# Indirect DMA transfers of a seven-layer kernel, issued one by one behind other engines' steps instead of 32 in a row

## The reference

```python
x = L0_attn_x
x = x + _L0_attn_ref(_layernorm(x, axis=-1), ...)   # linear ("cosformer") attention and an MLP
x = x + _L0_ffn_ref(_layernorm(x, axis=-1), ...)    # channel mix
x = x + _L1_attn_ref(_layernorm(x, axis=-1), ...)   # latent attention, causal softmax
x = x + _L1_ffn_ref(_layernorm(x, axis=-1), ...)    # two groups of 32 experts, the top 2 of each
x = x + _L2_attn_ref(_layernorm(x, axis=-1), ...)   # attention with rotary factors
x = x + _L2_ffn_ref(_layernorm(x, axis=-1), ...)    # 8 experts, top 2
x = x + _L3_attn_ref(_layernorm(x, axis=-1), ...)   # state-space layer
x = x + _L3_ffn_ref(_layernorm(x, axis=-1), ...)    # attention over heads, 8 gated experts
```

```python
order = jnp.argsort(flat_e)
tok = flat_t[order]
xs = x2[tok]
...
return jnp.zeros_like(x2).at[tok].add(ys)
```

## Time and profile before

| | |
|---|---|
| median of 3 runs | 6739.3 us (6714.13 to 6750.03) |
| the profiled execution: its time, its span | 6708.75 us, 6707.2 us |
| granted TensorE clock, mean | 0.802 |
| busy: PE, DVE, ACT, POOL | 4840.0, 3601.1, 1805.1, 2175.1 us |
| one pair of the first loop | 327.5 us (scatters start at 408.97 and 736.42) |
| one pair of the second loop | 443.8 us (fetches start at 3294.80 and 3738.62) |

### The profile page before, as it was taken

One profiled execution on the slowest core, in us unless ns is written; L12 is line 12 of the kernel. 1 busy time (PEld: TensorE's weight loads), 2 busy tenths in 40 slices (PEclk: granted clock), 3 DMA queues, 4 the chain that ended last, 5 costly groups with the idle time before them and its releaser, 6 DMA issues. The chain is left out here.

```text
span 6707.2 us, 94963 instructions
## 1 busy us (share of the span) xinstructions
PE 4840.0 (72%) x36264; PEld 2885.3 (43%) x36264; DVE 3601.1 (54%) x10874; ACT 1805.1 (27%) x2589; POOL 2175.1 (32%) x2704
## 2 busy tenths in 40 slices
PE   4969696969696868667768677686686676876763
PEld 2444444444444444443544435334444353443442
DVE  2645454545454545447456475374664754746644
ACT  1324242423232323233113132131231322312310
POOL 2222222222222222546225243262242531623424
PEclk9979797979797979887778867777787777876885
DMA  4000000000000000650000000000000000000000
GB/s 144 1 20 1 21 1 20 1 20 3 19 4 17 4 17 4 201 163 7 16 10 2 15 10 7 14 7 16 10 4 13 10 9 12 7 16 10 4 13 3
DMA packets 142050, 147.57 MB, mean 22 GB/s; under 512 B 31150, under 2 KB 126065, under 8 KB 141065
## 3 DMA queue, kind: packets, MB, share of 16 engines
q1 hardware_dynamic: 114424, 94.58, 4.8%
q0 software_dynamic: 18432, 37.79, 1.9%
q10 hardware_dynamic: 8736, 8.91, 0.4%
HBM read 70.75 MB, written 62.59 MB: 20 GB/s over the span
## 5 line engine op out<-in xcount | busy, mean ns | idle before, releaser
L772 DVE CUSTOM_DVE_ANT_0 twin<-twin,w_mask_row 128x512 f32<-128x512 f32 (+3 forms) x2048 | 953.8, 521 | 387.1 <-PE twin L1696 384.4
L1696 PE MATMUL twin<-arena 32*128 32x128 f32 (+3 forms) x4096 | 843.9, 536 | 57.1 <-DVE arena L772 30.5
L1714 PE MATMUL twin<-arena 32*128 32x128 f32 (+3 forms) x4096 | 800.6, 512 | 36.5 <-DVE arena L772 35.3
L1393 ACT ACTIVATE arena<-twin 128x768 f32<-128x768 f32 (+1 forms) x544 | 477.9, 882 | 724.4 <-PE twin L1725 387.4
L1714 PEld LDWEIGHTS twin<-arena 32*128 32x128 f32 x4096 | 367.5, 208 | 488.6 <-issue 289.9
L684 POOL TENSOR_SCALAR ve<-mv 128x4 f32<-128x4 f32 x128 | 27.7, 217 | 1566.9 <-DVE mv L732 1566.3
L1696 PEld LDWEIGHTS twin<-arena 32*128 32x128 f32 x4096 | 373.2, 213 | 233.4 <-issue 115.2
L687 POOL TENSOR_SCALAR ve<-ssq 128x4 f32<-128x4 f32 x80 | 24.9, 311 | 1147.3 <-DVE ssq L1238 604.5
L1649 PE MATMUL twin<-w_ident,b 128*128 128x128 f32 x328 | 91.3, 434 | 377.1 <-DVE b L753 326.8
L308 POOL DMA_INDIRECT sorted_x<-got,w_mo_first_slots x288 | 291.1, 1011 | 112.6 <-issue 86.5
L1737 PE MATMUL twin<-arena 128*32 128x128 f32 (+3 forms) x2944 | 309.3, 463 | 3.2 <-POOL arena L592 3.2
(11 more groups left out here) (440 smaller groups left out, 10823.2 us busy)
## 6 DMA issues: line engine op xcount, KB each, us to landing
sorted_y<-arena SPq DMA_DIRECT2D x96, 256.0 KB, 2.7
sorted_x<-zeros ACTq DMA_DIRECT2D x2, 4096.0 KB, 20.0
a<-sorted_x SPq DMA_DIRECT2D x64, 128.0 KB
b<-sorted_x SPq DMA_DIRECT2D x64, 128.0 KB, 2.3
hres<-sorted_x SPq DMA_DIRECT2D x64, 128.0 KB
sorted_x<-got,w_mo_first_slots POOLq DMA_INDIRECT x288
got<-sorted_y,back POOLq DMA_INDIRECT x288
x_out<-w_l_w SPq DMA_DIRECT2D x18, 256.0 KB, 2.3
```

The costliest lines, as they stand in the source:

```text
L772: last = dve.tensor_tensor_reduce(s[:, e, at:at + w], s[:, e, at:at + w], W["mask_row"][:, T - w:T], -1.0, 3e38, ALU.add, ALU.min, into)
L1393: act.activation(at_pt[tag][n % len(at_pt[tag])][:, :, 0:w], twin[SLOT["scores_t", c, u] % 3][:, :, 0:w], ACT.Exp, scale=1.0 if tag == "l1 ...
L1696: last = pe.matmul(s[:, e, at:at + w], queries[r, P * i:P * (i + 1)], keys[r, 0:w], start=(at == 0), stop=True, skip_group_check=True)
L1714: last = pe.matmul(s[:, e, at:at + w], keys[r, P * m:P * (m + 1)], queries[r, P * m:T], start=(at == 0), stop=(tag == "l2"), skip_group_ch ...
```

## The change

The functions keep what they transfer; only the place of each transfer in POOL's list changes. `send_rows` now takes a list of numbers. Of the 32 scatters, 16 are issued one by one behind the 16 signals `l0_probt` of linear attention, and 16 between the masks of latent attention, behind the second and the fifth of each quartet's six. Of the fetches, two come at the beginning of `l2_moe`, two behind the first norm of the state-space layer, eight behind the eight signals `l3_xc`, sixteen behind the eight signals `l3_decay`, two by two, and four behind the two norms of the last layer. The wait for `m_sent` and its `forget` (a DMA reset) move from before the masks of latent attention to the pair's end. In the experts' part the 32 scatters and 32 fetches stay in a row.

```diff
-        def send_rows(pool, sg):
+        def send_rows(pool, sg, numbers):
...
@@ the experts' part
-                        send_rows(pool, sg)
+                        send_rows(pool, sg, range(2 * SLOTS_OF_SEQ))
@@ l1_masks
                                 split(c + 1)
                                 for u in range(STEPS_OF):
                                     mask("l1", c, u)
+                                    if 0 <= c < QUARTETS and u % 3 == 1:
+                                        send_rows(pool, sg, (2 * QUARTETS + 2 * c + u // 3,))
@@ POOL's loop over layers and norms
                                 if (layer, of_layer) == (LAYERS - 2, 2):
-                                    pool.wait_ge(sg["m_back"], 16)
-                                    fetch_rows(pool, sg, range(2 * SLOTS_OF_SEQ))
+                                    for m in range(4 * len(PAIR)):
+                                        pool.wait_ge(sg["l3_xc"], m + 1)
+                                        fetch_rows(pool, sg, (4 + m,))
+                                    for m in range(NT * len(PAIR)):
+                                        pool.wait_ge(sg["l3_decay"], m + 1)
+                                        fetch_rows(pool, sg, (12 + 2 * m, 13 + 2 * m))
...
                                 if (layer, of_layer) == (0, 1):
-                                    send_rows(pool, sg)
+                                    for m in range(2 * QUARTETS):
+                                        pool.wait_ge(sg["l0_probt"], m + 1)
+                                        send_rows(pool, sg, (m,))
+                                if (layer, of_layer) == (LAYERS - 2, 0):
+                                    fetch_rows(pool, sg, (2, 3))
+                                if layer == LAYERS - 1:
+                                    fetch_rows(pool, sg, (28 + 2 * of_layer, 29 + 2 * of_layer))
                             if layer == L1_ATTENTION:
-                                pool.wait_ge(sg["m_sent"], 16 * 2 * SLOTS_OF_SEQ)
-                                forget(pool, sg["m_sent"])
                                 l1_masks()
...
                             if layer == L2_ATTENTION + 1:
                                 finish_norms()
+                                pool.wait_ge(sg["m_back"], 16)
+                                fetch_rows(pool, sg, (0, 1))
+                        if first <= L1_ATTENTION < last:
+                            pool.wait_ge(sg["m_sent"], 16 * 2 * SLOTS_OF_SEQ)
+                            forget(pool, sg["m_sent"])
```

12 lines of the change are left out of this document (6 added, 6 removed).

## The result

| | kernel before | changed kernel |
|---|---|---|
| median of the runs | 6726.7 us (6714.1 to 6750.0, 4 runs) | 6359.1 us (6351.9 to 6375.5, 4 runs) |
| profiled execution | 6708.75 us, span 6707.2 | 6351.87 us, span 6350.3 |
| granted TensorE clock, mean | 0.802 | 0.826 |

The ratio is 0.9435, with a 95% interval of 0.9395 to 0.9476: faster, as forecast. And the experiments further down add something that no trace of this pair of kernels could show: the stall that the change removes was there on one chip and not on three others. On two of those three the changed kernel was run too, and is slightly slower than the one before.

A forecast was written before the change was run, and what follows sets the result against it. Late hand-overs from PE beside POOL's bursts of transfers were taken to bound the kernel. Savings of 152 + 168 - 10 = 310 us from the 6739.3 us median gave 6429 us, forecast range 6386 to 6499; the 8-in-10 range was 6385 to 6590.

The forecast's parts named there:

- The place and the cause: Linear attention and state-space layer: hand-overs from PE come late beside POOL's bursts of 32 transfers; operations keep their length.
- the fetches: State-space layer: spreading them cuts the first sequence to 21.6 us, saving 21 us a pair, 168 us (bounds 145 and 176).
- the inner norms: Layers 6 and 7: two fetches between first and second norm cost 0.6 us, twice a pair, 10 us (bounds 0 and 24).
- the size of the state chain: Linear attention: spreading the first 16 scatters cuts the chain from 27.0 to 8 us, saving 152 us (bounds 134 and 162).
- The scatters between masks: Latent attention: 16 transfers of about 1.3 us fit POOL's 1.53 us idle before masks; cost 0, upper end 38 us.
- The rule that was weighed: Skill page: DMA traffic and compute can't slow each other, so late hand-overs would not be the transfers' doing and would stay.
- Half stays: Rival, both bursts: any transfer beside a chain of answers delays it, half of 320 us stays; 6589 us, chance 0.10.
- Each transfer carries its own delay: Rival, all 16 bursts: 1.1 us a transfer, so spreading adds 264 us, to 7013 us; chance 0.07.
- No change: Rival: state chain and gate input's bank are slow by themselves, transfers have nothing to do with it; 6749 us, chance 0.05.
- From about the fifteenth transfer on: Both bursts: the first 18 us or fourteen transfers disturb nothing, then PE's results reach others late, costing some 18.5 us.

The follow-up runs named there:

- e1: Changed kernel with the 32 fetches put back in one run, so only the scatters are spread; 6550.9 us, ratio 0.9727 to the kernel before.
- e2: Changed kernel with the 32 scatters put back in one run, so only the fetches are spread; 6578.5 us, ratio 0.9755 to the kernel before.
- e3: Kernel before, with one small POOL power behind each transfer of both runs of 32, nothing moved; 6392.6 us, ratio 0.9477.
- e13: Kernel before, unchanged, traced on chip C, where the stall is absent; 6330.5 us.
- e11: Changed kernel, unchanged, run on chip B; 6355.1 us, ratio 1.0025 to the kernel before there.
- e5: Kernel before, with 16 small POOL powers after the 10th and 20th transfer of both runs of 32; 6616.4 us, one run.
- e6: Changed kernel with all 32 scatters behind masks of latent attention and no fetch before an inner norm, chip A; 6363.8 us, ratio 0.9448.
- e14: Changed kernel, unchanged, run on chip C; 6346.9 us, ratio 1.0020 to the kernel before there.
- e8: Kernel before, with 20 fetches left in one run and twelve by fours behind the 1st, 3rd and 5th decay; 6660.2 us, one run.
- e7: Kernel before, with each state-space fetch taking 64 of its 128 rows; 6758.5 us, one run.
- e12: The kernel of e6 on chip B; 6351.3 us, ratio 1.0027 to the kernel before there.
- e10: Kernel before, with both runs of 32 started ten small POOL powers later, chip B; 6319.0 us, one run.
- e15: The kernel of e10 on chip C; 6327.1 us, one run.
- e17: The kernel of e10 once more on chip C; 6333.1 us, one run.
- e18: The kernel of e10 on chip D; 6352.7 us, one run, the kernel before 6326.6 us there.

## Why the prediction came out as it did

- **The place and the cause held, for the chip that was measured.** The stall sat in PE's hand-over during the runs of transfers, in two stages and nowhere else, and it went when the runs went. e1 and e2 show each edit at work alone, e3 shows that the run and not the place does it.
- **What the miss is made of.** The result is 380.2 us below the median that the prediction started from, and the sum was 310. Of the 70 us between them, 17.1 are linear attention (169.1 where 152 stood), 4.1 the fetches, 2.4 the inner norms, 23.3 the stages that no edit touches, and 23.4 the step from the profiled execution to the median.
- **The first step that failed is the size of the state chain.** It was put at 27.0 - 8 = 19 us a pair, 152 us, bounds 134 and 162. The chain takes 5.73 us, in the changed kernel and in e13 alike, 21.2 us less than before and 169.6 us in eight pairs. The two weighings (2.27 us) and the seven state operations, 0.49 us apart, are all of it. PE's matmuls and answers hide behind them entirely, where the prediction first added 1 us for them (6.8 us) and then went to 8 for the 3.25 us of the earlier trace rows. Those 12 matmuls stand behind a stop of 10.64 us, at a granted clock of 0.50; without the stop 16 of them take 2.23 us at 1.00. Behind the chain there is a second saving, which I counted for the fetches and forgot here: L1853's first two matmuls take 1.13 us and not 2.07, and from L1853 to the third weighing it is 1.7 us shorter on average. Against that, 1.7 us a pair are given back from the third weighing to the last. The stage gives 169.1 us.
- **The fetches: right.** Forecast 168, measured 172.1; 42.55 to 21.68 us where 21.6 stood.
- **The inner norms: right in kind.** 10 us forecast, 7.6 paid; DVE idles 0.5 us in place of 0.6.
- **The scatters between masks: right.** The stage is 0.5 us longer over eight pairs, and 0 was taken.
- **The second step that failed carried the result out of the range: no term for the clock, and the profile moved to the median as it stood.** With the edited stages alone, 333.6 us, the time would be 6739.3 - 333.6 = 6405.7 us, inside the range. Some 26 us of the 357 come from attention of the second loop, the ends of pairs and the last layer, which no edit touches. The 12.5 us of the ends may come with the change; the rest, as far as the traces tell, is luck (e11, the same kernel, has 1357.2 us in place of 1336.9 for the attention). And I moved the sum up by the 30.6 us that the profiled execution of before lay below its median, while that of the change lies 7.2 us below its own. (With its fourth run the kernel before has a median of 6726.7, and the 30.6 us become 18.) The range had 15 us for all this. The spread on chip A is 54 us (6709 to 6763), and single stages of one pair jump by 17 us.
- **The rule that was weighed.** By the Trainium skill, page "SBUF — State Buffer", section "SBUF: two separate sides", DMA traffic and compute can't slow each other, and the stops would have stayed. They went, from 17.65 to 0.69 us, so the rule did not decide here. What it says of ports is not refuted: weighings and states keep their lengths beside transfers (1.23 and 0.46 us in the earlier trace rows, and the same in the changed kernel). It was the signal from PE to its neighbours that was late. Whether the halts of PE in e5 have to do with ports, no run shows. On chips B, C and D the traces agree with the rule altogether.
- **The rivals.** "Half stays" is refuted by the table: the state-space stage is 753.1 us, 1.5 above the 751.6 of e13. "Each transfer carries its own delay" has a small true part: with the scatters by ones and twos signals of PE come up to 2.1 us late in the quartets (idle before L885 4.42 us and not 2.96), and linear attention is 652.7 us where e6, with no transfer in it, has 629.1. That is 24 us and not 264. On chip C the same transfers at the same places cost nothing there (629.0 us in e14). (The transfers from the fifteenth on are eighteen, not seventeen; that changes little.) "No change" is what happens on chips B and C, though not for the reason given: there the state chain and the bank are fast by themselves. The ratios, 1.0025 and 1.0020, are of the size of the change's own price.
- **"From about the fifteenth transfer on" describes the runs of 32, and is not a law.** In the runs of 32 at the old pace, in the kernel before and in e1 to e8, the first signal that is more than 1 us late falls beside the 10th to the 19th transfer: the 10th in four pairs of e8 and one of e7, the 18th for most fetches. In e5 it is the 8th of a run of twelve, and the halts of PE come in a run of ten, where it has many short matmuls to send. At the pace of e3 no signal is more than 1.0 us late.

A version that beats both everywhere was not found. e12 against e11 on one chip is 6351.3 to 6355.1 us, within the noise. On chip A it keeps the gain (0.9448, the changed kernel 0.9435 in its own group, so neither is shown to be better); on chips B and C the kernel before is the fastest by 0.2 to 0.3%.

## What to carry to other kernels

When a wait ends long after the work that it names, with both engines idle, look for what a third engine is doing in a run beside it, and take that away without moving anything (here by one small operation between transfers): it tells a held signal from a real dependence in one run. Before a signal is called late, look when the engine that waits for it starts, since its event may only be missing. Before tuning against such a stall, run the kernel on several chips, since a gain of 5.7% on one was a loss of 0.2% on others. And give the clock a term of its own in a prediction: the stages that an edit does not touch moved by 26 us here.

## What the runs showed of the hardware

- The same program, with the same transfers at the same pace, took 6709 to 6763 us on chip A and 6320 to 6360 us on chips B, C and D. In the profile before, PE's signal behind the first L2156 of a pair came 17 to 21 us late during back-to-back indirect transfers by GpSimd; in the traces of chips B, C and D none came more than 1 us late.
- On chip A neither a quarter of the bytes nor half of the rows of a transfer shortened the wait (17.33 and 22.76 us against 17.65); a power of 1.04 us behind each transfer did away with it (0.69 us).
- On chip A PE's issue of short matmuls itself falls during such a run: 88 in 12.5 us, against 243 in 15 us behind it. On chip C it was 194 in 6.2 us beside the same transfers.
- On chip A some of PE's semaphore events are missing from the traces though the signal came in time: 14 signals of L2192 in e8, where ACT starts 0.04 us after the matmul.
- A pair of latent attention takes 141 us at a granted clock of 0.97 or 158 us at 0.85, and nothing between, with the same matmuls; which one a pair gets differed from execution to execution of one program (none of the eight pairs in e10, e15 and e17, the first in e18).
